# A GNN with LSTM windows and a GCN layer: degrees as vector reductions in the prologue, and another order of GpSimd's lo parts and norms

## The reference, cut to what matters

```python
h = relu(layernorm(x))
h = relu(adj @ (h @ Wg0 + bg0));  h = relu(adj @ (h @ Wg1 + bg1))
for p in 1, 2, 3, 4:            # an LSTM over windows of p tokens, its last state
    h[:, p-1::p] = lstm_last(windows(h, p))      # replaces the window's last token
x = x + h
h = relu(layernorm(x))
A = adj + I;  deg = A.sum(0) + A.sum(1) - diag(A);  A_hat = A * deg^-.5[:, None] * deg^-.5
out = batchnorm(relu(batchnorm((A_hat @ h) @ W1.T + b1)) @ W2.T + b2)   # over all tokens
x = x + out
```

## Time and profile before

| | |
|---|---|
| runs | 571.85, 573.59, 573.43 us; median 573.43 |
| profiled execution | 574.75 us, span 572.9, mean granted clock 0.976 |
| TensorE busy | 514.4 us (90%), weight loads 439.0 |
| DVE, ScalarE, GpSimd busy | 423.3 (74%), 355.6 (62%), 194.6 (34%) |
| chain that ended last | PE 48%, issue 21%, DVE 11%, POOL 9%, ACT 6% |

### The profile page before, as it was taken

The page is one execution under the profiler, slowest core; times in us unless marked ns, Lnnn a source line. Parts: engine busy times, 40 slices in busy tenths (PEclk is TensorE's granted clock), DMA queues, the critical chain, the costliest instruction groups (busy, mean ns, idle before and its releaser), DMA issues.

```text
span 572.9 us, 8138 instructions
## 1 busy us (share of the span) xinstructions
PE 514.4 (90%) x2761; PEld 439.0 (77%) x2761; DVE 423.3 (74%) x974; ACT 355.6 (62%) x679; POOL 194.6 (34%) x299
## 2 busy tenths in 40 slices
PE   3998999698989999999999999999869998895866
PEld 3787778597988788989987889899657898773546
DVE  3656666787876888778568887775686888877867
ACT  2544755464568666667586666676766777446864
POOL 5402003413310457137003562350033515146941
PEclk9999899798999999999999999999999999998997
DMA  8300020000001110202021101010730000500007
GB/s 233 100 19 2 0 93 18 2 18 1 20 18 38 55 38 37 76 1 74 1 93 54 40 37 57 1 55 1 292 131 18 19 2 20 189 32 0 1 2 293
DMA packets 17838, 31.22 MB, mean 54 GB/s; under 512 B 1498, under 2 KB 6020, under 8 KB 17796
## 3 DMA queue, kind: packets, MB, share of 16 engines
q1 hardware_dynamic: 16804, 30.17, 15.5%
q10 hardware_dynamic: 992, 0.52, 0.3%
HBM read 19.16 MB, written 11.53 MB: 54 GB/s over the span
## 4 chain that ended last, share of the span: by engine, by line
PE 48%; issue 21%; DVE 11%; POOL 9%; ACT 6%; POOLq 3%; DMA 1%; DVEq 0%; ACTq 0%
PE gate_ps L1086 10%; PE gate_ps L1087 9%; PE gate_ps L1088 9%; PE pre_ps L1087 4%; PE pre_ps L1088 4%; PE pre_ps L1086 4%; POOL x_pre L368 3%; PE post_ps L1086 3%; POOL z_back L423 3%; PE post_ps L1088 2%; PE post_ps L1087 2%; POOLq L366 2%; ACT gate L644 2%; ACT gate L634 1%; DVE cell L929 1%
## 5 line engine op out<-in xcount | busy, mean ns | idle before, releaser
L634 ACT ACTIVATE gate<-gate_ps,gate_bias 128x256 f32<-128x256 f32 (+2 forms) x312 | 164.8, 564 | 46.6 <-PE gate_ps L1088 44.9
L1086 PE MATMUL gate_ps<-by_class_hi,wih_hi 128*128 128x256 f32 (+2 forms) x264 | 86.3, 327 | 12.9 <-POOL by_class_lo L387 7.2
L644 ACT ACTIVATE gate<-cell 128x512 f32<-128x512 f32 (+2 forms) x88 | 45.3, 515 | 69.2 <-DVE cell L924 35.9
L1088 PE MATMUL gate_ps<-by_class_lo,wih_hi 128*128 128x256 f32 (+2 forms) x264 | 84.5, 320 | 0.0
L1087 PE MATMUL gate_ps<-by_class_hi,wih_lo 128*128 128x256 f32 (+2 forms) x264 | 84.4, 320 | 0.0
L1086 PEld LDWEIGHTS gate_ps<-by_class_hi,wih_hi 128*128 128x128 f32 x264 | 50.7, 192 | 20.1 <-POOL by_class_lo L387 8.1
L1086 PE MATMUL gate_ps<-hstep_hi,whh_hi 128*128 128x256 f32 (+2 forms) x192 | 60.8, 317 | 0.0
L1087 PE MATMUL gate_ps<-hstep_hi,whh_lo 128*128 128x256 f32 (+2 forms) x192 | 60.7, 316 | 0.0
L1088 PE MATMUL gate_ps<-hstep_lo,whh_hi 128*128 128x256 f32 (+2 forms) x192 | 60.6, 315 | 0.0
L387 POOL TENSOR_TENSOR by_class_lo<-h,by_class_hi 128x256 fp32r<-128x256 f32 (+1 forms) x40 | 35.4, 892 | 58.4 <-ACT by_class_hi L642 58.4
L358 POOL TENSOR_TENSOR ln_pre<-mv_pre,eps 128x4 f32<-128x4 f32 x16 | 5.1, 316 | 144.7 <-DVE mv_pre L796 144.7
(11 more groups left out here) (310 smaller groups left out, 1375.2 us busy)
## 6 DMA issues: line engine op xcount, KB each, us to landing
x_pre<-in_x SPq DMA_DIRECT2D x16, 256.0 KB, 2.7
x<-in_x SPq DMA_DIRECT2D x16, 256.0 KB, 2.8
z_spill<-z_ring SPq DMA_DIRECT2D x8, 512.0 KB, 2.7
z_back<-z_spill SPq DMA_DIRECT2D x8, 512.0 KB, 6.7
x_spill<-x SPq DMA_DIRECT2D x12, 256.0 KB, 2.1
x_back<-x_spill SPq DMA_DIRECT2D x1, 3072.0 KB, 11.0
out<-x_back SPq DMA_DIRECT2D x12, 256.0 KB, 2.1
x<-in_adj SPq DMA_DIRECT2D x1, 1024.0 KB, 6.5
```

Of the source, the lines that this page charges most:

```text
L634: nc.scalar.activation(gate[:, tile_of(g), gt, 0:size], gate_ps[k % GATE_BANKS][:, 0:size], ACT.Tanh if gt == G_GATE else ACT.Sigmoid, bia ...
L644: nc.scalar.activation(gate[:, tile_of(g), G_GATE, 0:size], cell[:, tile_of(g), 0:size], ACT.Tanh)\
L1086: nc.tensor.matmul(ps, w[0], m[0], start=start, stop=False)
L1088: return nc.tensor.matmul(ps, w[0], m[1], start=False, stop=stop)
```

## The change

Four edits go together. The degrees are no longer summed by matmuls: in the prologue DVE reduces along the free dimension the raw adjacency, the hi and the lo part of its transpose, and the masked diagonal; GpSimd combines the four, adds one and takes the power. For that the raw adjacency is loaded with four neighbouring rows to a partition, and the transposes write every fourth PSUM column. The steps that follow the degrees move to earlier slots, and SP's loads wait for the fourth reduction. The prologue's first entries are reordered: bank 0 and norm 0 ahead of the statistics of batch 1. GpSimd's norms of slot s come behind the lo part of slot s + 1 where that slot makes one (`NORMS_AFTER`). The W2 stage is not touched.

```diff
-DEG_SUM, DEG_TOKENS, DEG_POW, DINV_DIAG, DINV_ROWS = 3, 3, 4, 5, 7
-HAT_CHUNK = (8, 11, 14, 17)
+DINV_DIAG, DINV_ROWS = 2, 4
+HAT_CHUNK = (5, 9, 12, 17)
+DEG_ROWS, DEG_HI, DEG_LO, DEG_DIAG = range(4)
...
+def makes_parts(slot):
+
+    return slot < N_SLOTS and TURNS[slot][2] >= 3 and TURNS[slot][3] + 1 < TURNS[slot][2]
+
+
+NORMS_AFTER = [[at for at in (slot - 1, slot) if at >= 0 and makes_parts(at + 1) == (at < slot)] for slot in range(N_SLOTS)]
...
-        PROLOGUE = ([("stats", 0), ("stats", 1), ("bank", 0), ("norm", 0), ("bank", 1), ("bank", 2), ("bank", 3),
+        PROLOGUE = ([("stats", 0), ("bank", 0), ("norm", 0), ("stats", 1), ("bank", 1), ("bank", 2), ("bank", 3),
...
-                     ("bank", 7), (LIN1, 0), (LIN1, 1), (LIN0, 2), ("bank", 8), (AGG0, 3), (AGG1, 0), ("bank", 9),
-                     (LIN0, 3), (LIN1, 2), (AGG1, 1), ("bank", 10)]
+                     ("bank", 7), (LIN1, 0), (LIN1, 1), (LIN0, 2), ("bank", 8), ("deg", DEG_ROWS), (AGG0, 3), ("deg", DEG_HI), (AGG1, 0), ("bank", 9),
+                     (LIN0, 3), (LIN1, 2), ("deg", DEG_LO), (AGG1, 1), ("bank", 10)]
...
-                    + [(LIN1, 3), ("bank", 11), (AGG1, 2), ("bank", 12)]
+                    + [(LIN1, 3), ("bank", 11), ("deg", DEG_DIAG), (AGG1, 2), ("bank", 12)]
...
+            pool.wait_ge(deg_ready, 4)
+            nc.gpsimd.tensor_tensor(deg[:, DEG_ROWS, :], deg[:, DEG_ROWS, :], deg[:, DEG_HI, :], ALU.add)
+            nc.gpsimd.tensor_tensor(deg[:, DEG_LO, :], deg[:, DEG_LO, :], deg[:, DEG_DIAG, :], ALU.subtract).then_inc(deg_sum, 1)
+            pool.wait_ge(deg_sum, 1)
+            nc.gpsimd.tensor_tensor(deg[:, DEG_ROWS, :], deg[:, DEG_ROWS, :], deg[:, DEG_LO, :], ALU.add).then_inc(deg_sum, 1)
+            pool.wait_ge(deg_sum, 2)
+            nc.gpsimd.tensor_tensor(deg[:, DEG_ROWS, :], deg[:, DEG_ROWS, :], ones_f[:, 0:CHUNKS], ALU.add).then_inc(deg_sum, 1)
+            pool.wait_ge(deg_sum, 3)
+            nc.gpsimd.tensor_tensor(dinv[:, :], deg[:, DEG_ROWS, :], minus_half[:, :], ALU.pow).then_inc(dinv_ready, 1)
...
-                for kind, n in PRE_AFTER[slot]:
-                    if kind == "stats":
-                        norm_pre(n)
-                for kind, n in POST_AFTER[slot]:
-                    if kind == "stats":
-                        norm_post(n, y_post)
-                if slot == DEG_POW:
-
-                    pool.wait_ge(deg_ready, 1)
-                    nc.gpsimd.tensor_tensor(dinv[:, :], deg[:, :], minus_half[:, :], ALU.pow).then_inc(dinv_ready, 1)
+
+                for at in NORMS_AFTER[slot]:
+                    for kind, n in PRE_AFTER[at]:
+                        if kind == "stats":
+                            norm_pre(n)
+                    for kind, n in POST_AFTER[at]:
+                        if kind == "stats":
+                            norm_post(n, y_post)
...
-            sp.dma_start(adj_raw[:, :, :], adj.rearrange("(c p) s -> p c s", p=P)).then_inc(adj_in, 16)
+            sp.dma_start(adj_raw[:, :, :], adj.rearrange("(p c) s -> p c s", c=CHUNKS)).then_inc(adj_in, 16)
...
-                    sp.wait_ge(deg_mm, 1)
+                    sp.wait_ge(deg_ready, 4)
...
+            def deg_part(i):
+
+                if i == DEG_DIAG:
+                    dve.wait_ge(consts_ready, 3)
+                    for c in range(CHUNKS):
+                        last = nc.vector.tensor_tensor(deg_fix[:, c, :], adj_raw[:, c, c::CHUNKS], ident[:, :], ALU.mult)
+                    last.then_inc(diag_part, 1)
+                    dve.wait_ge(diag_part, 1)
+                if i == DEG_HI:
+                    dve.wait_ge(setup_hi, CHUNKS)
+                if i == DEG_LO:
+                    dve.wait_ge(setup_lo, CHUNKS)
+                src = {DEG_ROWS: adj_raw, DEG_HI: adj_t[0], DEG_LO: adj_t[1], DEG_DIAG: deg_fix}[i][:, :, :]
+                if i in (DEG_HI, DEG_LO):
+                    src = f32(src)
+                nc.vector.reduce_sum(deg[:, i, :], src, AX.X).then_inc(deg_ready, 1)
...
-                    if i == len(BANKS) - 1:
-
-                        dve.wait_ge(adj_in, 16)
-                        dve.wait_ge(consts_ready, 3)
-                        for c in range(CHUNKS):
-                            last = nc.vector.tensor_tensor(deg_fix[:, c, :], adj_raw[:, c, c * P:(c + 1) * P],
-                                                           ident[:, :], ALU.mult)
...
-                if n == DEG_TOKENS:
-
-                    dve.wait_ge(deg_mm, 1)
...
-                        last = nc.tensor.transpose(ps[:, c * P:(c + 1) * P], adj_raw[:, c, i::CHUNKS], ident[:, :])
+                        last = nc.tensor.transpose(ps[:, c::CHUNKS], adj_raw[:, c, i::CHUNKS], ident[:, :])
...
             def deg_steps(n):
-                if n == DEG_SUM:
-
-                    pe.wait_ge(fix_ready, 1)
+                if n == DINV_ROWS:
+
+                    pe.wait_ge(dscale_ready, 1)
                     pe.wait_ge(pre_lo, 4 * EARLY)
-                    for c in range(CHUNKS):
-                        nc.tensor.matmul(post_ps[:, :], ones_f[:, :], adj_raw[:, c, :], start=c == 0, stop=False)
-                        for part in adj_t:
-                            nc.tensor.matmul(post_ps[:, :], ones_r[:, :], part[:, c, :], start=False, stop=False)
-                    for c in range(CHUNKS):
-                        last = nc.tensor.matmul(post_ps[:, c * P:(c + 1) * P], ones_f[:, :], deg_fix[:, c, :],
-                                                start=False, stop=c == CHUNKS - 1)
-                    last.then_inc(deg_mm, 1)
-                if n == DINV_ROWS:
-
-                    pe.wait_ge(dscale_ready, 1)
```

More of the change, by code:

```diff
@@ L179, in build @@
         dinv = sb("dinv", [P, CHUNKS])
-        deg = sb("deg", [P, CHUNKS])
+        deg = sb("deg", [P, 4, CHUNKS])
         hat = pair("hat", [P, CHUNKS, T])
@@ L250, in build @@
         wg_hi, wg_ready = sem("wg_hi"), sem("wg_ready")
-        fix_part, fix_ready, deg_mm, deg_part, deg_ready = (
-            sem("fix_part"), sem("fix_ready"), sem("deg_mm"), sem("deg_part"), sem("deg_ready"))
+        diag_part, deg_ready, deg_sum = sem("diag_part"), sem("deg_ready"), sem("deg_sum")
         dinv_ready, dscale_ready, dinv_mm, hat_part, hat_ready = (
@@ L602, in _ @@
                     normed(i, x_pre[:, i % 2, :], nrm[i % 2], pre_y, pre_nhi)
-                elif kind != "stats":
+                elif kind not in ("stats", "deg"):
                     pre_unit(kind, pre_number(i, kind), i, prologue_ps(i), i % 2)
@@ L819, in _ @@
                     bank_lo(i)
-                    if i == len(BANKS) - 1:
-                        dve.wait_ge(adj_in, 16)
-                        dve.wait_ge(consts_ready, 3)
-                        for c in range(CHUNKS):
-                            last = nc.vector.tensor_tensor(deg_fix[:, c, :], adj_raw[:, c, c * P:(c + 1) * P],
-                                                           ident[:, :], ALU.mult)
-                        last.then_inc(fix_part, 1)
-                        dve.wait_ge(fix_part, 1)
-                        for c in range(CHUNKS):
-                            last = nc.vector.tensor_tensor(deg_fix[:, c, :], ident[:, :], deg_fix[:, c, :],
-                                                           ALU.subtract)
-                        last.then_inc(fix_ready, 1)
+                elif kind == "deg":
+                    deg_part(i)
                 elif kind == "rows":
@@ L874, in hat_steps @@
             def hat_steps(n):
-                if n == DEG_TOKENS:
-                    dve.wait_ge(deg_mm, 1)
-                    for c in range(CHUNKS):
-                        last = nc.vector.tensor_tensor(hat_t[:, c * P:(c + 1) * P], post_ps[:, c::CHUNKS],
-                                                       ident[:, :], ALU.mult)
-                    last.then_inc(deg_part, 1)
-                    dve.wait_ge(deg_part, 1)
-                    nc.vector.reduce_sum(deg[:, :], hat_t[:, :].rearrange("p (c q) -> p c q", c=CHUNKS), AX.X)\
-                        .then_inc(deg_ready, 1)
                 if n == DINV_DIAG:
@@ L1155, in _ @@
                     bank(i)
-                elif kind not in ("stats", "norm", "rows"):
+                elif kind not in ("stats", "norm", "rows", "deg"):
                     if kind == LIN0 and i == 0:
@@ L1186, in deg_steps @@
             def deg_steps(n):
-                if n == DEG_SUM:
-                    pe.wait_ge(fix_ready, 1)
-                    pe.wait_ge(pre_lo, 4 * EARLY)
-                    for c in range(CHUNKS):
-                        nc.tensor.matmul(post_ps[:, :], ones_f[:, :], adj_raw[:, c, :], start=c == 0, stop=False)
-                        for part in adj_t:
-                            nc.tensor.matmul(post_ps[:, :], ones_r[:, :], part[:, c, :], start=False, stop=False)
-                    for c in range(CHUNKS):
```

(4 more changed lines are left out.)

## The result

The changed kernel takes **568.99 us** (median of 10 runs, 566.94 to 570.75) against 573.21 us for the kernel before (10 runs taken beside them). The ratio is 0.9921 with a 95% interval of 0.9896 to 0.9945: faster by 4.2 us.

What follows compares the result with a forecast made beforehand. TensorE was taken as nearly full in rounds 1 to 3, with slack in round 0; gains of 0.9 (opening), 6.6 (round 0) and 0.3 (later) sum to 7.8 us, giving a median of 565.6, range 561.8 to 570.3.

Steps and rivals of the forecast that it cites:

- two rivals: Less gained, new waits bringing a half-clock stretch: 569.0, chance 0.22; more gained, half-clock stretches not occurring: 562.2, chance 0.10.
- The removed matmuls: Degree sums at 71.50 to 77.61 leave TensorE's path: at most 6.1 us, not all at once.
- The reductions: DVE's prologue reductions, 2.3 us each for three, 8.5 us with the rest, hidden in 15.3 us idle: price 0.
- The layout: Adjacency load with 8 KB rows could take 5.4 us, 1.1 less; priced 0, kept 0 to -1.1.
- The opening order: Norm 0's lo part ahead of batch 1's statistics, first aggregation earlier: 0.9 us, bounds 0 and 1.1 more.
- The transposes: 16 opening transposes, now writing every fourth PSUM column, still take 3.7 us: price 0.
- rival 4: Strided transposes in the opening slow the kernel; at four times as long 3.3 us more, 576.7; chance 0.03.
- Round 0: With the matmuls gone and GpSimd's lo part ahead of the norm, turn 12 starts 6.6 us earlier, opening left out.
- the wait of 2.3 us ahead of batch 5's second linear layer: Behind turns 10 and 11, TensorE idle some 2.3 us because hat chunk 1 on DVE holds turn 10's products.
- rival 1: New waits of turns 8 to 11 bring a half-clock stretch, 2.5 lost, chunk 0 0.9 longer: 569.0; chance 0.22.
- The chunk at slot 5: Hat chunk 0, before at slot 8, follows turn 5's hstep lo on DVE, 3.0 to 3.2 us; turn 8 waits 1.9.
- The later rounds: Rounds 1 to 3: norms start one lo part later, remaining GpSimd waits shrink: 0.3 us gained, bounds 0 and 2.3.

Runs made afterwards that it cites:

- the reorder alone: The kernel before with only GpSimd's queue changed (norms behind the next slot's lo part): 573.35 us against 573.02.
- the layout alone: The kernel before with only the adjacency load in rows of 8 KB and the strided transposes: 572.15 us against 573.43.
- the two edits together: The changed kernel with the hat chunks and dinv in their old slots and the norms reordered in round 0 only: 566.01 us against 573.43.

## Why the prediction was right, and where not

The median of 568.99 lies in the range, 3.4 us above the 565.6. The account of the two profiled executions, in spans: 2.2 us gained in the opening, 6.3 more up to turn 12, 0.3 to the end of round 0, then 1.0 lost up to 472, 0.9 more up to 490, and 1.4 in the tail. That is 5.6 of the 7.8, and the median moved by 4.2. The range was 8.5 us wide because it took in two rivals, and several terms of the sum missed and offset one another, so that the median lies in it is in part luck.

- **The removed matmuls: right.** Turn 4 follows turn 3 without a block of ones, at 69.33.
- **The reductions: right in size, and hidden, but with less room than I wrote.** They took 2.276, 2.274, 2.275 and 0.686 us against my 2.3 and 0.69, the diagonal products 1.25 in all. But "15.3 us in which DVE was idle" was read over 40 us; where the reductions stand 9.6 us were idle, and 2.1 are left. GpSimd's five operations end at 51.4 (four of 0.20 and one of 1.33, where I had taken 1.00 for each).
- **The layout: the step that was mis-sized.** My estimate of 5.4 us for the load came out (5.4 in two profiles, 5.2 in two others), but I priced it at 0. It is worth 3.2 us at the LSTM's start (the reorder alone, which changes nothing there, is 0.5 ahead by chance), because the load delayed the one behind it too. My question "what is queued behind" was asked of GpSimd and not of this queue.
- **The opening order: the wrong sign.** I read the 0.97 us wait as the order's doing; the layout alone removes it, and the order costs 1.0 at the LSTM's start. By luck the two together are 2.2, near the 2.0 at the ends of my bounds.
- **The transposes: rival 4 is refuted.** 3.69 us before and after, median 417 and 418 ns. The rule of the Trainium skill, "SBUF — State Buffer", section "Door 1: The DMA port swizzle", that non-contiguous PSUM access slows matmuls, isn't borne out here for writes of every fourth column.
- **Round 0: 6.3 against 6.6**, turn 8 4.1 against 4.2, turn 10 6.8 against 6.7 (opening taken off). The wait of 1.9 ahead of turn 8 was 1.28 in one profile and 0.75 in the other. Two errors cancel in the sum: the wait of 2.3 us ahead of batch 5's second linear layer did not come, and a half-clock stretch of 6.80 us (97.80) did, which I had assumed away. It begins in the new wait ahead of turn 10. This is half of rival 1, whose 569.0 is the measured number, but by another sum.
- **The chunk at slot 5: followed correctly, never weighed.** I worked out what each chunk delays and didn't ask whether it had to be there: with the old slots the kernel is 2.5 us faster.
- **The later rounds: the step that failed.** "I take 0.3, bounds 0 and 2.3" allowed no loss. I had named the next lo part, about 1 us later, and priced it at 0 because DVE was nearly as late. The runs show 1.8 us lost in rounds 1 to 3. Half of it goes at slot 81, where the order moves a wait of 1.9 us from one turn to the next three and GpSimd's lo parts fall on DVE's chain; the other half goes in steps of 0.1 to 0.3 us, two of them at waits for z_ring.
- **The tail: not foreseen.** Nothing in it was changed. In the profiles of the three kernels that keep the degree matmuls it lasts 82.3 to 82.4 us (from the transposes behind the last turns, 490.58 in the kernel before, to the end), in the eleven others 83.0 to 84.2. The loss is not TensorE's. It is in the stores of the output, kernel before and then changed kernel:

```profile
529.61 0.50 PE L1086 MATMUL gate_ps<-hid_hi,w_hi 128*128 128x512 f32 x1 [0.93 <-DVE hid_lo L747]
...
559.44 8.12 SPq L528 DMA_DIRECT2D out<-x_back  x12
567.02 0.76 PE L1320 MATMUL gate_ps<-ident,z_back 128*128 128x128 f32 x5
567.82 2.36 SPq L528 DMA_DIRECT2D out<-x  x4
```

```profile
522.65 0.41 PE L1099 MATMUL gate_ps<-hid_hi,w_hi 128*128 128x512 f32 x1
...
552.39 8.54 SPq L545 DMA_DIRECT2D out<-x_back  x12
559.65 0.77 PE L1322 MATMUL gate_ps<-ident,z_back 128*128 128x128 f32 x5
560.98 2.69 SPq L545 DMA_DIRECT2D out<-x  x4
```

A longer half-clock stretch (514.2 to 521.0, where the kernel before has 522.1 to 525.5) takes 1.1 us from the changed kernel's lead, but the kernel before then waits 0.93 us at 529.61 where the changed one does not wait (522.65), and the lead is back at 7.0. At the first output store it is 7.05, at the last five matmuls 7.37, at the end of the span 5.6. From the first store's issue to the end all three kernels with the degree matmuls take 13.49 us, the changed kernel 14.90 and the ten others without them 14.2 to 15.4; one store takes 2.9 and 3.5 us from issue to landing (medians of the twelve and of the four) where it took 2.1 and 2.8. The layout alone and the reorder alone are among the three, so neither brings it. What else in the change slows the stores stays open.

## What to carry to other kernels

When an instruction is moved earlier, ask who reads its result and what chain it is put in front of: here three of the four hat chunks were brought forward on the engine that sets the pace, for a reader some 100 us away, at 2.5 us. A transfer that becomes shorter also frees whatever stands behind it in its queue, which here was worth as much as the transfer itself. And "hidden" is a number: compare the added work with the idle time of the same stretch, since one more helping of the same work cost 5 us. A lead that is lost need not be lost in one place, and the end of the last matmul is not the end of the kernel: compare both.

## What was new about the hardware

- The lower clock comes in stretches of 3.4 or 6.8 us (granted 0.50 in all windows inside); where TensorE is busy throughout, that is up to 1.7 or 3.4 us each. Some begin in a wait of TensorE (97.8 in the changed kernel), and they are not at the same places in two executions of one kernel. Over thirteen of the profiles here they make 8.3 to 19.0 us of an execution (the span times what the mean granted clock lacks of 1). In some kernels they go with the spread of the runs (560.5 us at 0.985, 568.1 at 0.970 for the two edits together), but not in the ten runs of the changed kernel (565.1 at 0.977, 568.9 at 0.978).
- The granted clock on record isn't always the time: the profile of the reorder alone reads 0.95 where the others read 1.00, its mean is 0.935, and yet its matmuls of 256 columns take 0.283 us as in the others, and its run of 573.60 us stands beside one of 573.59 at 0.983.
- DVE's tensor-tensor operations are held by GpSimd's. In the changed kernel's trace 21 of those of 128 x 256 start while GpSimd makes a lo part. The 17 that start 0.37 us or more before its end all end 0.28 us behind it (0.65 to 0.96 us long, against 0.42); the four that start 0.11 before its end take 0.43. Those that lie inside one of GpSimd's norm operations (tensor-scalar) take 0.41. An order of GpSimd's queue therefore changes DVE's chain, even where nobody waits for GpSimd.
- The load of 1 MB took 5.4 us in rows of 8 KB and 6.5 in rows of 2 KB, and what stood behind landed 2.2 us sooner.
